# Moving stack transfers between queues, reordering the head of each batch, and taking the last group's scores by key tile

## What is computed

```
x = x + attn(bi_wkv(x, fside, fside, w1, u1, cond), w_qkv, w_o)
x = x + ffn(bi_wkv(x, fside, fside, w2, u2, cond), w_gate, w_up, w_down)

bi_wkv: a_t = a_(t-1) * decay + exp(k_t) * v_t     b_t = b_(t-1) * decay + exp(k_t)
        forward and backward over t, then sigmoid(r) * num / den * gain
attn:   softmax over causal keys of q k^T / sqrt(32), times v, times w_o^T
ffn:    (silu(q(x) gate) * (q(x) up)) -> quantised -> down
```

## Time and profile before

| | |
|---|---|
| median of 3 runs | 870.95 us (870.93 to 872.39) |
| the profiled execution, its own time | 873.02 us |
| its span | 871.3 us |
| PE busy | 741.5 us (85%) |
| DVE busy | 752.6 us (86%) |
| ACT busy | 507.6 us (58%) |
| chain that ended last, by engine | DVE 44%, PE 26%, issue 13%, ACT 8%, DMA 3%, SPq 3% |
| POOL's first issue of `stack(b, 1)`, behind `down_ready` | batch 1 at 344.92, batch 2 at 525.45, batch 3 at 706.25 us |

### The profile page before, as it was taken

One profiled execution on the slowest core, in us unless ns is written; L12 is line 12 of the kernel. 1 busy time (PEld: TensorE's weight loads), 2 busy tenths in 40 slices (PEclk: granted clock), 3 DMA queues, 4 the chain that ended last, 5 costly groups with the idle time before them and its releaser, 6 DMA issues.

```text
span 871.3 us, 10845 instructions
## 1 busy us (share of the span) xinstructions
PE 741.5 (85%) x3964; PEld 393.8 (45%) x4001; DVE 752.6 (86%) x1070; ACT 507.6 (58%) x754; POOL 72.6 (8%) x149
## 2 busy tenths in 40 slices
PE   4567668699889999798899998988899998999785
PEld 1222223355544444454444443555444444557674
DVE  4899999999999879789998798899898888834887
ACT  4966655376874575378764663677736636443440
POOL 1000001202000003011000021110000211200000
PEclk9786687899999999999999999999999999999998
DMA  9623210557100005654010047460100355500001
GB/s 325 266 96 109 101 63 23 125 124 182 39 30 21 1 12 128 190 163 102 13 37 1 13 97 205 113 166 14 37 1 12 83 153 135 126 1 1 1 2 48
DMA packets 31252, 73.06 MB, mean 84 GB/s; under 512 B 5856, under 2 KB 6880, under 8 KB 29408
## 3 DMA queue, kind: packets, MB, share of 16 engines
q1 hardware_dynamic: 19584, 46.67, 17.9%
q0 software_dynamic: 6144, 16.79, 8.1%
q10 hardware_dynamic: 5472, 8.92, 3.2%
HBM read 34.61 MB, written 4.19 MB: 45 GB/s over the span
## 4 chain that ended last, share of the span: by engine, by line
DVE 44%; PE 26%; issue 13%; ACT 8%; DMA 3%; SPq 3%; POOL 1%; ACTq 0%; DVEq 0%
PE bank L1627 9%; DVE negmax L1077 5%; DVE num L983 3%; SPq L337 3%; PE bank L1520 2%; DVE fn L969 2%; PE bank L1464 2%; PE bank L1482 2%; PE bank L1392 2%; ACT region L583 2%; DVE ratio L1116 2%; PE bank L1426 2%; PE bank L1493 2%; DMA stacks<-rows 1%; DVE den L994 1%
## 5 line engine op out<-in xcount | busy, mean ns | idle before, releaser
L1077 DVE TENSOR_REDUCE negmax<-bank 128x4 f32<-128x512 f32 (+2 forms) x96 | 97.8, 1036 | 31.9 <-PE bank L1429 19.5
L583 ACT ACTIVATE region<-bank 128x384 f32<-128x384 f32 (+1 forms) x192 | 93.2, 526 | 46.3 <-PE bank L1467 45.4
L1464 PE MATMUL bank<-stacks 128*128 128x512 f32 (+3 forms) x256 | 103.2, 411 | 18.8 <-ACT region L583 13.4
L1400 PE MATMUL bank<-h,wqkv 128*128 128x512 f32 x256 | 115.5, 605 | 0.0
L1426 PE MATMUL bank<-stacks 128*128 128x128 f32 (+3 forms) x256 | 78.6, 402 | 7.1 <-DVE negmax L1077 4.9
L337 POOL DMA_DIRECT2D stacks<-rounded_rows x64 | 34.7, 550 | 521.1 <-DVE ratio L1116 321.6
L1400 PEld LDWEIGHTS bank<-h,wqkv 128*128 128x128 f32 x256 | 49.4, 195 | 58.1 <-issue 57.2
L1466 PE MATMUL bank<-maxrow,pick 128*128 128x384 bf16 (+3 forms) x236 | 73.2, 310 | 0.0
L1464 PEld LDWEIGHTS bank<-stacks 128*128 128x128 f32 x256 | 50.3, 197 | 45.0 <-ACT region L583 27.4
L1392 PE MATMUL bank<-wqkv,h 128*128 128x512 f32 x128 | 62.7, 635 | 4.7 <-DVE h L1017 4.7
L1682 PE MATMUL bank<-region,ident 128*128 128x512 f32 x64 | 49.2, 930 | 12.0 <-DVE identb L928 12.0
(11 more groups left out here) (197 smaller groups left out, 1558.5 us busy)
## 6 DMA issues: line engine op xcount, KB each, us to landing
stacks<-rounded_rows SPq DMA_DIRECT2D x64, 128.0 KB, 4.5
stacks<-rounded_rows POOLq DMA_DIRECT2D x64, 128.0 KB, 5.0
stacks<-rows SPq DMA_DIRECT2D x64, 128.0 KB, 2.5
stacks<-rows POOLq DMA_DIRECT2D x64, 128.0 KB, 2.6
kt<-in_fside ACTq DMA_DIRECT2D x30, 256.0 KB, 3.3
region<-in_w_gate SPq DMA_DIRECT2D x4, 1024.0 KB, 11.3
h<-in_x SPq DMA_DIRECT2D x4, 1024.0 KB, 5.7
xt<-in_x SPq DMA_DIRECT2D x4, 1024.0 KB, 5.6
```

The source lines that it names most:

```text
L583: nc.scalar.activation(probs[:, i, P_AT[tiles[0]]:P_AT[tiles[0]] + columns], key_bank(g, n)[:, 0:columns], ACT.Exp, scale=SCALE).then_inc( ...
L1077: nc.vector.tensor_reduce(o, scored, AX_X, ALU.max, negate=True).then_inc(max_taken, 1)
L1400: mm = nc.tensor.matmul(qk_banks(g)[s][:, :], wqkv[:, j, C * s + P * g:C * s + P * g + P], h[:, j, :], start=(j == 0), stop=(j == CJ - 1))
L1464: nc.tensor.matmul(o, ks[s][:, i, P * t:P * t + P], qs[s][:, i, P * t:T], start=True, stop=False, skip_group_check=True)
```

## The change

It has eight edits.

1. SP sends only head 0 of `stack(b, 1)`, and before the outputs of batch b - 1 (now a function `store`, called behind it). ACT sends head 1, once `down_ready` has come. POOL sends heads 2 and 3 as before.
2. ACT copies the turned maxima of group 0 before the scalings of unit 2, and the values of tile 0 after two exponentials.
3. On DVE `add_own(b, 9)` goes behind the additions of the down projection.
4. On DVE, for b > 0, the first four maxima come before `forward` of unit 2, not mixed with it.
5. On PE the projections of group 2 are cut, two of the first four steps ahead of the first scores, and the values go behind the scores.
6. ACT loads its function table before `load_k(b, 4)` and `floored(b, 4)`, not after.
7. The last group's score units go by key tile over all four heads: `key_unit` gives head n % 4, tile n // 4.
8. The last group's weighing waits, for each of the first three key tiles, for that tile's four exponentials; `cap_exp(b, 7)` goes behind all twelve exponentials.

```diff
+        def key_unit(g, n):
+            if g == GROUPS - 1:
+                return n % HG, KEY_TILES[n // HG]
+            return n // PER_HEAD, KEY_TILES[n % PER_HEAD]
...
             def turn(b, more):
                 sp.wait_ge(down_ready, 1 + b)
-                stack(sp, b, 1, 0, 2)
+                stack(sp, b, 1, 0, 1)
                 if b:
+                    store(b - 1, True)
                     sp.wait_ge(stored, b * (16 * CJ))
...
                 low_parts(b, 1)
+                act.wait_ge(down_ready, 1 + b)
+                stack(act, b, 1, 1, 2)
                 load_k(b, 1)
...
                 late_high_parts(b)
+                copy_maxima(b, 0)
                 weigh(b, 2, 0)
                 weigh(b, 2, 1)
-                copy_maxima(b, 0)
+
+                exps(b, 0, 0, 2)
                 copy_values(b, (0,))
-
-                exps(b, 0, 0, 5)
+                exps(b, 0, 2, 5)
...
                 copy_maxima(b, 2)
+                if more:
+                    table(6)
                 load_k(b, 4)
                 floored(b, 4)
-                if more:
-                    table(6)
...
-                exps(b, 3, 2, 9)
+                exps(b, 3, 2, 12)
                 cap_exp(b, 7)
-                exps(b, 3, 9, 12)
...
-                    pe.wait_ge(p_ready, b * (GROUPS * UNITS) + g * UNITS + UNITS)
+                    if g < GROUPS - 1:
+                        pe.wait_ge(p_ready, b * (GROUPS * UNITS) + g * UNITS + UNITS)
                 for t in range(first, last):
+                    if g == GROUPS - 1 and t < PER_HEAD:
+                        pe.wait_ge(p_ready, b * (GROUPS * UNITS) + g * UNITS + HG * (t + 1))
...
                     pe.wait_ge(raw_copied, 2 * b + 1)
-                    project_qk(b, 2, 0)
+                    project_qk(b, 2, 0, 0, 2)
                     scores(b, 0, 0)
                     scores(b, 0, 1)
-                    project_qk(b, 2, 1)
+                    project_qk(b, 2, 0, 2)
                     scores(b, 0, 2)
                     scores(b, 0, 3)
-                    project_values(b, 0, 0, 2)
+                    project_qk(b, 2, 1)
                     scores(b, 0, 4)
                     scores(b, 0, 5)
+                    project_values(b, 0, 0, 2)
```

More of the change, by code:

```diff
@@ L379, in turn, with store @@
                     stack(sp, b + 1, 0, 0, 2)
+            def store(b, more):
                 for j in range(CJ):
@@ L392, in _ @@
                 turn(b, b + 1 < B)
+            store(B - 1, False)
             sp.wait_ge(weights_in, 32)
@@ L579, in exps @@
                 for n in range(first, last):
-                    i, tiles = n // PER_HEAD, KEY_TILES[n % PER_HEAD]
+                    i, tiles = key_unit(g, n)
                     columns = sum(CAUSAL[t] for t in tiles)
@@ L1231, in turn @@
             def turn(b, more):
-                if b:
-                    forward(b, 2, 0)
-                    maxima(b, 0, 0)
-                    maxima(b, 0, 1)
-                    forward(b, 2, 1)
-                    maxima(b, 0, 2)
-                    maxima(b, 0, 3)
-                else:
-                    maxima(b, 0, 0)
-                    maxima(b, 0, 1)
+                maxima(b, 0, 0)
+                maxima(b, 0, 1)
+                if b == 0:
                     backward(b, 1, 1)
                     add_own(b, 1)
-                    maxima(b, 0, 2)
-                    maxima(b, 0, 3)
-                    forward(b, 2, 0)
-                    forward(b, 2, 1)
+                maxima(b, 0, 2)
+                maxima(b, 0, 3)
+                forward(b, 2, 0)
+                forward(b, 2, 1)
                 maxima(b, 0, 4)
@@ L1373, in turn @@
                 backward(b, 9, 1)
-                add_own(b, 9)
                 for j in range(CJ):
@@ L1377, in turn @@
                     nc.vector.tensor_tensor(xt[:, j, :], bank[j][:, :], xt[:, j, :], ALU.add).then_inc(out_ready, 1)
+                add_own(b, 9)
             for b in range(B):
@@ L1395, in project_values, with project_qk @@
                     mm.then_inc(v_ready, 1)
-            def project_qk(b, g, s):
-                for j in range(CJ):
+            def project_qk(b, g, s, first=0, last=CJ):
+                for j in range(first, last):
                     mm = nc.tensor.matmul(qk_banks(g)[s][:, :], wqkv[:, j, C * s + P * g:C * s + P * g + P], h[:, j, :],
-                                          start=(j == 0), stop=(j == CJ - 1))
-                mm.then_inc(qk_ready, 1)
+                                          start=(j == 0), stop=(j == CJ - 1), skip_group_check=True)
+                if last == CJ:
+                    mm.then_inc(qk_ready, 1)
             def leave_low(b, g, s):
@@ L1445, in scores_by_key @@
             def scores_by_key(b, g, n):
-                s, i, tiles = g % 2, n // PER_HEAD, KEY_TILES[n % PER_HEAD]
+                s, (i, tiles) = g % 2, key_unit(g, n)
                 if n == 0:
```

## The result

The changed kernel takes 858.25 us (median of 4 runs, 857.08 to 858.31), beside 871.11 us (4 runs, 870.93 to 872.39) for the kernel before on the same chip. The ratio is 0.9846, with a 95% interval of 0.9829 to 0.9863. The prediction was 857.1 us. The profiled execution took 857.08 us, with a span of 855.3 us.

What follows compares the result with a forecast made beforehand. It took each later batch's head, waiting for stacks behind outputs, as the bound, with DVE pacing most attention in batches 0 to 2. 3.6 + 8.7 + 0.85 + 0.7 = 13.9 us off 870.95 gave 857.1 us; range 853.5 to 865 us.

Steps and rivals of the forecast that it cites:

- The head's stretch: Batches 1 to 3, first to second split of the maxima: earlier stacks bring it to 19.01 us, 8.7 us in all.
- The split sooner: DVE before each head's first split: 1.4 us of waiting replaces 2.59, so 1.2 us sooner, 3.6 us for three heads.
- Batch 3's scores of group 2: PE after batch 3's second split: these scores start 3.02 us behind it instead of 3.87, 0.85 us gained.
- The last weighing: End of batch 3: PE starts weighing the last group without waiting for the twelfth exponential, 0.7 us gained.
- ACT's issues, edit 6: ACT's four new DMA issues fit its idle time in the head, and the earlier table load gains nothing: 0 each.
- The stacks as late as before: Rival: DMA engines are already full, so stacks land no sooner; 866.6 us, chance 0.15 for this or nearly so.
- The clock rival: PE's clock falls again in the heads, each giving back 1.9 us: 859.0 to 862.8 us; chance 0.20 for one or two.

Runs made afterwards that it cites:

- PE's old order: The changed kernel with edit 5 alone undone, so PE does whole projections ahead of the scores again while DVE keeps its new order: 871.17 us, ratio 0.9981.

## Why the prediction was right, point by point

**The head's stretch, 8.7 us: right in mechanism and size.** It measured 8.8 us, with 19.00 us in each batch, as batch 0 had told. The landing came at 11.4 us behind POOL's first issue in batch 2; the estimate was 12.6, and the bounds reached from 11.2 to 15.0. The two parts of that term could be told apart. In heads with outputs first and a clock of 1.00 the stretch is 21.25 to 22.13 us (the kernel before in batch 2 and three heads of the experiments), so late stacks cost 2.2 to 3.1 us. Where PE's clock falls with early stacks (one head of edits 1 and 2 alone, and all three with PE's old order), the stretch is 20.45 to 21.96 us, 1.5 to 3 us for the clock alone. The forecast counted 1.9 us of it once, in batch 1, and it was won. But it had not looked at the clock in batch 3. The three stretches of the kernel before:

```profile
359.21:382.40 23.19, 19.74 (x106) 11.80 (x112) 17.56 (x21) 15.53 (x27) 4.22 (x8) 0.93 0.51 138
539.73:560.98 21.25, 18.16 (x106) 10.46 (x112) 17.37 (x21) 15.53 (x27) 4.22 (x8) 1.00 0.52 142
720.54:741.86 21.32, 19.59 (x106) 11.05 (x112) 17.37 (x21) 15.53 (x27) 4.22 (x8) 0.92 0.50 135
```

In batch 3 the clock is as low as in batch 1 and hardly costs anything. PE's transposes and the four matmuls right behind the split take 1.4 us longer there than in batch 2, and PE's wait for the copy of the maxima behind them is 1.4 us shorter (0.62 for 1.98 us). So in that head the fallen clock took up time in which PE would have waited for the late stacks anyway.

**The split sooner, 3.6 us: right, a little large.** 0.89 us in each head, 2.7 in all. The term took 1.4 us of waiting for 2.59; it is 1.22 ahead of the additions, and 0.35 us for slot 4, which I had held to be ready. What the prediction did not say is that this term and the one before are not independent. Edits 3 to 5 make the kernel 1% slower as long as the stacks are late, and all edits but the first together are worth nothing that can be measured.

**Batch 3's scores of group 2, 0.85 us: this step failed.** They start 3.94 us behind the second split (3.87 before), and PE still waits for a DMA:

```profile
730.81 0.41 PE L1432 MATMUL bank<-stacks 128*128 128x128 f32 x2 [0.85 <-DMA stacks<-rows]
```

That these stacks would move against the split was wrong. In all fourteen profiled kernels the scores start 3.47 to 4.03 us behind the second split in batch 3, after a wait of 0.38 to 0.94 us for these stacks, with early and with late stacks of group 1 alike. I read it so that the split and the stacks both follow PE's score units; no run tests that. The same wait did go in batch 2, where nothing had been forecast (0.70 us of the table). Before, PE waited there like this:

```profile
565.22 0.41 PE L1426 MATMUL bank<-stacks 128*128 128x128 f32 x2 [1.15 <-DMA stacks<-rows]
```

In the changed kernel it starts 3.02 us behind the split, with no such wait. But neither has any of the twelve other kernels in batches 0 to 2, those with late stacks included. So this wait is most likely a thing of the one execution of the kernel before that was profiled, and the 0.70 us is not shown to be the change's.

**The last weighing, 0.7 us: right, and a little small.** 0.94 us in the changed kernel, 0.96 for these edits alone. PE now starts the weighing without a wait. In batches 0 to 2 it waits 1.05 us for `normalise` (estimate 1.4) and, as forecast, that brings nothing by itself. What I left out was batch 2's wait for the sums, 1.15 us, and it went. The experiments make an accident unlikely. In the three kernels without edits 7 and 8 PE stands 2.58 us ahead of this weighing, and in 4 of their 9 places DVE then waits 0.15 to 1.15 us for the sums. In two of the four the weighing's first eight matmuls took 1.82 and 1.93 us, at a fallen clock; in the other two they took 1.06, so its first piece doesn't show it there. In the eleven kernels with edits 7 and 8 PE stands 1.05 us, and none of 33 places has the wait.

**ACT's issues, edit 6: 0.** ACT's four issues took 3.1 us and delayed nothing that can be measured: without them the time is the same. Edit 6 was not tried by itself.

**The rivals.** "The stacks as late as before" was priced at 866.6 us, 4.3 us less than the kernel before. Edit 1 undone takes 872.5 us on a chip on which the kernel before takes 873.0. So its mechanism is real, and its gain was too large by about 4 us: the 1.2 us a head that edit 2 was to give back did not come. Counted from the split, the rounded copies start 2.3 to 2.8 us behind it, where it was 0.8 to 1.1, because the split comes 0.9 us sooner and the stacks land 0.3 to 1.1 us later still; the copy of the maxima stands 4.2 to 4.7 us behind the split, where it was 3.9 to 4.3. The Trainium skill (DMA: Bandwidth & Descriptors, "Issuing engines are not separate DMA queues") spoke for that rival, and about ACT's queue it is right: without ACT's issues the time is 858.15 us, the same within the noise. It did not decide the case, since the gain was in the order. The clock rival did not come in the changed kernel: 1.00 in the first stretch of every batch.

The sum of the forecast was 13.9 us. Its four terms measure 8.8, 2.7, 0 and 0.9 us in the traces, 12.4 in all; the medians differ by 12.9. The two profiled executions differ by 16.0. The rest of that is the start (1.3 us) and batch 2's 1.55 and 0.70 us, which the profile before had and its other batches had not. The forecast's sum counted none of these. That its total came within 1.2 us of the measured time is in part luck: two of its terms were 1.75 us too large, and something that it did not count, which traces of one execution can't assign, made up a part of that.

## What to carry to other kernels

When DMA engines are full, look for transfers that nobody waits for and issue them behind the ones that somebody waits for; a further issuing engine is no substitute. Price an edit on a path together with the wait that ends last there: the reordering of DVE and PE alone (edits 3 to 5) costs 1% with late stacks, while with early ones edits 3 to 8 together bring 0.6% (0.9902 to 0.9846). Where several batches run the same steps, one of them that lacks the disturbance tells what removing it will bring. And when work is put into a wait, the question is not how long that wait is, but which of the following items is ready at that moment.

## What the hardware showed that I had not expected

A few microseconds of an idle PE can cost nearly as much again afterwards. PE's waits of 0.38 us ahead of the transposes were followed by a granted clock of 1.00 in every head whose stacks were early (21 heads of seven kernels); those of 3.50 us by 0.85 to 0.92, between the levels of 1.2 and 2.4 GHz, each time. Waits of 2.15 us stand there in nine heads (the kernel before, edits 1 and 2 alone, edits 7 and 8 alone), and in two of them the matmuls right behind were slow already. With early stacks the price was 1.5 to 3 us a head. It is not a constant of the clock, as batch 3 of the kernel before showed above.

An issue of a DMA on SP is no constant. In batch 2 its median was 0.60 us in the changed kernel and 0.65 in the kernel before, where the longest took 2.25; it was 0.84 us with eight stacks on SP ahead of the outputs, and 2.2 us when outputs and two other queues' stacks were in flight, while POOL's stayed at 0.53.
